# Two pieces of shared-expert work moved ahead of the routed experts, with the additions and weight loads that follow from it

## The reference

```python
x = x + xattn(layernorm(x), ctx, mask, Wq, Wk, Wv, Wo)
h = layernorm(x)                                     # 4096 rows of 512
topk_idx, topk_w = gate(h)                           # 4 of 32 experts a token, 2 of 4 groups
out = moe(h, topk_idx, topk_w, w1, w2, w3)           # 32 experts, inner width 256, 128 rows each
shared = silu(h @ shared_gate) * (h @ shared_up) @ shared_down   # inner width 512
x = x + out + shared
```

## Time and profile before

| | |
|---|---|
| median of 3 runs | 1642.79 us |
| the profiled execution, its own time | 1645.73 us |
| its span, first to last instruction | 1644.0 us |
| PE busy | 1602.1 us, 97% |
| DVE busy | 1216.7 us, 74% |
| ACT busy | 827.0 us, 50% |
| POOL busy | 818.7 us, 50% |
| mean share of the 16 DMA engines, 1397.75 to 1576.01 us | 0.93 |

### The profile page before, as it was taken

The page is one execution under the profiler, slowest core; times in us unless marked ns, Lnnn a source line. Parts: engine busy times, 40 slices in busy tenths (PEclk is TensorE's granted clock), DMA queues, the critical chain, the costliest instruction groups (busy, mean ns, idle before and its releaser), DMA issues. The chain is left out here.

```text
span 1644.0 us, 34926 instructions
## 1 busy us (share of the span) xinstructions
PE 1602.1 (97%) x12194; PEld 1149.3 (70%) x12194; DVE 1216.7 (74%) x3510; ACT 827.0 (50%) x2050; POOL 818.7 (50%) x1130
## 2 busy tenths in 40 slices
PE   7999999999999999999999999999999999999994
PEld 4767777777777686777777777777777777666641
DVE  7987676767767676767677778787787766687883
ACT  5764443534344443444354454544454443777782
POOL 3444554536354645445455564646464456354453
PEclk9999999999999999999999999999999999999997
DMA  8754433434334333434354545545444476899984
GB/s 242 186 142 84 82 81 78 96 67 98 69 88 72 88 76 78 85 78 85 69 120 79 105 96 114 113 87 108 91 108 87 104 260 181 266 280 292 301 209 59
DMA packets 395053, 205.69 MB, mean 125 GB/s; under 512 B 347888, under 2 KB 356080, under 8 KB 394880
## 3 DMA queue, kind: packets, MB, share of 16 engines
q1 hardware_dynamic: 380720, 181.32, 44.8%
q0 software_dynamic: 13600, 21.10, 6.9%
q10 hardware_dynamic: 560, 1.05, 0.2%
HBM read 87.67 MB, written 32.41 MB: 73 GB/s over the span
## 5 line engine op out<-in xcount | busy, mean ns | idle before, releaser
L980 ACT ACTIVATE arena<-arena,neg_max 128x256 f32<-128x256 f32 x512 | 253.7, 496 | 379.5 <-DVE neg_max L1297 319.0
L716 POOL TENSOR_SCALAR arena<-arena,prob_scale 128x256 f16<-128x256 f32 x384 | 183.4, 492 | 454.0 <-DVE prob_scale L1306 452.2
L1656 PE MATMUL ps_query<-xn_both,arena 128*128 128x256 f16 x1024 | 279.8, 273 | 1.5 <-DMA xn_both<-xn_half 1.5
L1657 PE MATMUL ps_query<-xn_both,arena 128*128 128x256 f16 x1024 | 279.8, 273 | 0.0
L1658 PE MATMUL ps_query<-xn_both,arena 128*128 128x256 f16 x1024 | 279.8, 273 | 0.0
L1297 DVE CUSTOM_DVE_ANT_0 arena<-ps_score,mask_add 128x256 f32<-128x256 f32 x512 | 186.7, 420 | 120.6 <-PE ps_score L1658 119.7
L1312 DVE SCALAR_TENSOR_TENSOR arena<-arena,prob_scale 128x256 f16<-128x256 f32 x384 | 231.7, 651 | 7.6 <-POOL arena L716 7.6
L1656 PE MATMUL ps_out<-arena,o_t 128*128 128x512 f16 x512 | 194.1, 379 | 4.2 <-DVE o_t L1317 4.2
L1657 PE MATMUL ps_out<-arena,o_t 128*128 128x512 f16 x512 | 194.0, 379 | 0.0
L1658 PE MATMUL ps_out<-arena,o_t 128*128 128x512 f16 x512 | 194.0, 379 | 0.0
L771 POOL DMA_INDIRECT slot_table<-entry,slot_at x128 | 132.9, 1039 | 48.1 <-issue 33.6
(11 more groups left out here) (341 smaller groups left out, 4067.8 us busy)
## 6 DMA issues: line engine op xcount, KB each, us to landing
arena<-w SPq DMA_DIRECT2D x96, 512.0 KB, 6.7
x_in<-x SPq DMA_DIRECT2D x15, 512.0 KB, 4.1
xn_rows<-xn_half SPq DMA_DIRECT2D x15, 512.0 KB
out_rows_dram<-x SPq DMA_DIRECT2D x30, 256.0 KB
ctx_in<-ctx_t SPq DMA_DIRECT2D x16, 256.0 KB, 3.0
weight_in<-wq SPq DMA_DIRECT2D x8, 512.0 KB, 5.1
weight_in<-wo SPq DMA_DIRECT2D x8, 512.0 KB, 4.4
arena<-arena SPq DMA_TRANSPOSE x256
```

The source lines that it names most:

```text
L716: pool.tensor_scalar(p_rows[:, c, 0, :], probs[:, c, :], prob_scale[:, c:c + 1], 1.0, ALU.mult, ALU.mult).then_inc(norm_hi, 1)
L980: act.activation(probs[:, c, :], probs[:, c, :], ACT.Exp, bias=neg_max[:, c:c + 1], scale=-1.0, accum_out=prob_sum[:, c:c + 1]).then_inc(e ...
L1656: pe.matmul(dst, a.hi, b.hi, start=start and n == 0, stop=False)
L1657: pe.matmul(dst, a.hi, b.lo, start=False, stop=False)
```

## The change

EARLY goes from 24 to 26: the pieces 24 and 25, both halves of the down product of late sequence 3, run ahead of expert 0, and every later piece runs beside an expert two earlier. Experts 22 to 31 are then without a piece. The rule for add_in is written anew, since sequence 3 has no piece beside an expert any more; its table becomes {4: (3,), 12: (4, 5), 22: (6, 7)}. Late sequences 1 and 2 become separate groups of additions, so that add_shared(2) now waits for the landing of add_shared(1), and piece 24 for that of add_shared(1) alone. POOL splits pieces up to EARLY - 1 in a loop; the two new ones are down pieces and need no split. SP loads the experts 6, 7 and 8 whole, one after the other, where it staggered the parts. DVE makes the low halves of expert 1 right after piece 11 and those of expert 2 behind pieces 14, 15 and 16.

```diff
--- before.py
+++ after.py
@@ -62,7 +62,7 @@
     PIECES += [("d", _n - 1, t) for t in range(TB)] if _n else []
     PIECES += [("u", _n, f) for f in range(2, FSB)]
 PIECES += [("d", len(LATE) - 1, t) for t in range(TB)]
-EARLY = 24
+EARLY = 26
 RAMP = 18
 NOT_BY_POOL = (10, 11, 14, 15, 16)
 BESIDE = {}
@@ -445,14 +445,14 @@
 
 
         additions = [("s", n) for n in range(1, 3)]
-        add_in = {max(e + e % 2, 4): ns for ns in ((3,), (4, 5), (6, 7)) for e, k in BESIDE.items()
-                  if PIECES[k] == ("d", ns[-1], TB - 1)}
+        staged_in = {PIECES[k][1]: e for e, k in BESIDE.items() if PIECES[k][0] == "d"} | {3: 0}
+        add_in = {max(staged_in[ns[-1]] // 2 * 2 + 2, 4): ns for ns in ((3,), (4, 5), (6, 7))}
         for e in range(2, E + 1, 2):
             additions += [("s", n) for n in add_in.get(e, ())]
             additions += [("x", e - 1), ("x", e - 2)]
         assert len(additions) == E + len(LATE) - 1
         adds_done, adds_before, total = {}, {}, 0
-        for kind, together in groupby(additions, key=lambda what: (what[0], what[1] // 2 if what[0] == "x" else 0)):
+        for kind, together in groupby(additions, key=lambda what: (what[0], what[1] // 2 if what[0] == "x" else min(what[1], 3))):
             together = list(together)
             size = 16 * len(together) * (TB if kind[0] == "s" else 1)
             for what in together:
@@ -622,9 +622,12 @@
             load_x2t(4)
 
 
-            for e in range(AHEAD - 2, E):
+            for e in range(AHEAD, AHEAD + HELD):
                 for part in range(3):
-                    if e + 2 - part >= AHEAD:
+                    load_expert(e, part)
+            for e in range(AHEAD, E):
+                for part in range(3):
+                    if e + 2 - part >= AHEAD + HELD:
                         load_expert(e + 2 - part, part)
                 if AHEAD <= e < AHEAD - 1 + KEPT:
                     load_x2t(e - AHEAD + 5)
@@ -751,7 +754,7 @@
                     pool.wait_ge(staged, TB * n + t + 1)
                     if t == 0:
                         pool.wait_ge(out_rows, 16 * TB * (LATE[n] + 1))
-                        if n > 2:
+                        if n > 1:
                             pool.wait_ge(added, adds_before["s", n])
                     pool.dma_start(out[r:r + P, :], shared_y[n % 2][t], accum_op=ALU.add).then_inc(
                         added if n else added_first, 16)
@@ -850,7 +853,7 @@
             add_shared(2)
             for e in range(4, 6):
                 gather(e)
-            for k in (22, 23):
+            for k in range(22, EARLY):
                 late_split(k)
             pool.wait_ge(out_rows, 16 * TB * B)
             pool.wait_ge(added_first, 16 * TB)
@@ -1607,16 +1610,12 @@
             pick(position)
             find_slots(z)
             piece_rest(10)
-            for k, e, part in ((11, 0, 2), (14, 1, 0), (15, 1, 1), (16, 1, 2)):
+            for k, lows in ((11, ((0, 2), (1, 0), (1, 1), (1, 2))), (14, ((2, 0),)), (15, ((2, 1),)), (16, ((2, 2),))):
                 piece(k)
-                if k > 11:
-                    expert_low(e, part)
                 piece_rest(k)
-                if k == 11:
+                for e, part in lows:
                     expert_low(e, part)
             piece(17)
-            for part in range(3):
-                expert_low(2, part)
             piece(20)
             dve.wait_ge(in_table, 16)
             dve.tensor_scalar(slot_weight[:, :], table[:, :, 1].bitcast(F32), 0.5 * GLU * GLU * HE_S / ROUTE_SCALE,
@@ -1625,7 +1624,7 @@
             dve.wait_ge(table_scaled, 2)
             dve.tensor_scalar(to_spare, row_f, spare_row[:, 0:1], -PAIR_S / EY_S, ALU.subtract, ALU.mult).then_inc(
                 table_scaled, 1)
-            for k in (21, 22, 23):
+            for k in range(21, EARLY):
                 piece(k)
             for e in range(E + 1):
                 if e < E:
```

## The result

The changed kernel took 1650.35 us (median of 20 runs, 1644.61 to 1656.67), the kernel before 1642.82 us beside it (20 runs, 1639.11 to 1648.58). The ratio is 1.0045, 95% interval 1.0035 to 1.0054: slower by 7.4 us. Forecast were +4.2 us and slower as the likeliest; the time lies inside the range of 1641.5 to 1651.0, at its upper end, and just outside the forecast's own range of 1644.5 to 1650.

What follows compares the result with a forecast made beforehand. From 1498.54 the serial chain of POOL's additions sets the end. Its links summed to a span of 1648.2 against 1644.0, + 4.2 us; added to the median 1642.79 this gave 1647.0 us, range 1641.5 to 1651.0.

Steps and rivals of the forecast that it cites:

- Two pieces ahead, + 5.18: PE in front of the experts: two down pieces of 2.59 us each start expert 0 5.18 us later, at 1402.93.
- Experts 22 and 23 without pieces, + 1.01: PE at experts 22 and 23: the pair takes 10.79 us against 9.78 of own work, losing 1.01 us.
- The chain never catches up: POOL's additions: each group starts later than its data from expert 10 on; backlog 7.0 us at experts 18 and 19.
- the first rival: Additions of experts 12 to 19: links fall to 12.33 us, the chain meets its data, end 1637.7; chance 0.20.
- a start by 1578: Sign in POOL's chain: sequences 6 and 7 starting by 1578, not near 1583, means it caught up and the forecast is wrong.
- The moved step takes nothing out of the chain: Shared step of sequences 6 and 7, expert 24 to 22: the chain must pass it all the same, no saving.
- The link behind the sequences 6 and 7, 9.73: Chain from the start of sequences 6 and 7 to pair 20 and 21: 9.73 us, 1583.1 to 1592.8.
- the link *to* the step: Chain from experts 18 and 19 to sequences 6 and 7: taken as 13.5 us, between 15.47 and 9.56.
- SP and DVE, cost 0: Earlier loads of experts 6 to 8 and moved low halves: no gain by themselves, no piece moved, cost 0.
- the third rival: PE at piece 24 stalls for piece 21's halves beyond 1.8 us of slack; 4 us late gives 1649.2; chance 0.15.
- The second rival (late links long by chance): Late chain links: ordinary ones 14.05, the one ahead of sequences 6 and 7 11.6; 1643.7, no change; chance 0.15.
- Links long by the load alone: Chain links between pairs: 14.52 us while weights stream in against 8.17 without, read as the effect of DRAM load.

Runs made afterwards that it cites:

- after: First profile of the changed kernel itself: the profiled execution took 1648.54 us; the kernel's median was 1650.35 us, ratio 1.0045 against before.
- e1: Changed kernel with SP's loads and DVE's low halves in the order of before: ratio 1.0023 against before, median 1650.35 us.
- e10: Changed kernel with POOL's split of piece 20 ahead of the four gathers and that of piece 21 between second and third: 1.0027, 1650.93 us.
- e3: Changed kernel once more, unedited, for its own time and a second profile: ratio 1.0043 against before, median 1653.43 us.
- e4: Changed kernel with both additions of every pair of experts issued back to back, no gather between: ratio 1.0016 against before, 1649.46 us.
- e5: Kernel before with both additions of every pair of experts issued back to back, no gather between: ratio 0.9976 against before, 1645.29 us.
- e7: Changed kernel without the additions of late sequences 6 and 7, their shared part missing from the output: ratio 0.9999 against before, 1650.87 us.
- e9: Kernel before once more, same code, for a second profile: one execution of 1641.85 us.
- e6: Changed kernel with the additions of sequences 6 and 7 back at expert 24, behind experts 20 and 21: ratio 1.0028 against before, 1654.17 us.
- e8: Kernel before with pair additions back to back and late sequences 4 to 7 added singly at experts 8, 14, 20, 24: 0.9963, 1644.54 us.

## Why the prediction was right, and too small

- **Two pieces ahead, + 5.18.** Held. Expert 0 starts 5.8 us later after the first late piece than before in after, stall of 1.51 us included, and 4.7 later in e1 and e10, which have no stall. From the first late piece to experts 8 and 9's addition it is 163.8 us against 159.1, + 4.7.
- **Experts 22 and 23 without pieces, + 1.01.** Held: from expert 22 to expert 24 it is 10.7 us on PE (1564.9 to 1575.6; forecast 10.79).
- **The chain never catches up.** Held in the profile of after, where every group from expert 10 on was later than its data, and not in e3, where the chain met its data at experts 16 to 19, as the first rival had it (in e4 and e5 as well, with pairs back to back). On the forecast's scale the sequences 6 and 7 started at 1583.1 in after and at 1577.0 in e3; the prediction itself called a start by 1578 a sign that it is wrong. Of the 6.2 us that e3 had won by then over after, 3.1 were left at the end: the longer links behind the step took the rest. The first rival's price, 9.3 us, was too high for that reason.
- **The moved step takes nothing out of the chain.** Held: it must still pass it, and without it (e7) the loss is gone.
- **The link behind the sequences 6 and 7, 9.73: the term that was mis-sized.** I took it from the earlier trace rows, where the step stood at expert 24, behind the last weights. At expert 22 it stands ahead of their end. Measured were 11.92 to 14.61, 13.3 on average over the five profiles, + 3.6 us. The prediction named this too as a sign of being wrong, links behind the step that are not 8 to 10 us. I had asked that question of the link *to* the step, and took 13.5 (measured 13.28 in after), but not of the link behind it, though the earlier trace rows have one for the same four transfers inside the weight stream: that of the sequences 4 and 5, 12.67.

That term does not account for the 7.4 us, since others fell by as much. The parts in us, for the five profiles with the sequences 6 and 7 together at expert 22 (after and e3 are the changed kernel itself, the others have one edit each):

| part | forecast | after | e3 | e1 | e4 | e10 | mean of five |
|---|---|---|---|---|---|---|---|
| first late piece to experts 8, 9 | 164.3 | 163.8 | 163.6 | 162.6 | 164.1 | 162.7 | 163.3 |
| to the sequences 6, 7 | 93.8 | 94.4 | 88.4 | 94.9 | 87.6 | 89.9 | 91.0 |
| link behind them | 9.7 | 11.9 | 12.9 | 14.4 | 14.6 | 12.7 | 13.3 |
| from there to the end | 55.4 | 53.6 | 55.8 | 55.0 | 54.8 | 54.6 | 54.8 |
| sum | 323.2 | 323.7 | 320.6 | 326.9 | 321.0 | 319.8 | 322.4 |

The sum was right to 1 us on average, and in after to 0.5, while its terms were off by up to 3.6 in either direction; that part is luck. The two profiles of the changed kernel average 322.2 us, the two of before (319.0 and, in e9, 317.1) 318.1: + 4.1, beside the forecast's + 4.2, though the profiles of one kernel differ by 2 to 3 us. The medians say 7.4. The profiled executions of the changed kernel were faster than its medians (1648.54 against 1650.35, 1649.75 against 1653.43), so where the other 3 us lie is open.

- **SP and DVE, cost 0.** Not held beside the two pieces: the slot table came later in every profile with the new orders, and PE stalled at piece 24 by 0.7 us (e3) and 1.51 us (after), as the third rival said from a slack of 1.8 us. In after PE reached piece 24 71.0 us after the first late piece (forecast 71.9) and the halves of piece 21 were ready after 72.3 (forecast 70.1). That rival and the forecast happened together; I had priced them as cases that exclude each other. Whether the new orders cost more than the stall is open.
- **The second rival (late links long by chance).** Half right as a caution: the profile of before was 2.9 us over the median, and e9 puts its time from the first piece 1.9 us lower.
- **Links long by the load alone.** The prediction set 14.52 us under load against 8.17 without and gave the difference to the load. But the pairs of 14.52 have a gather between their additions and those of 8.17 have none. Back to back and still under load a pair's link was 8.8 to 12.6 us, 11.0 on average, so a part of the difference goes with the gather.
- e6, which moves only the step back, gives back 0.15 to 0.17%, in the direction of the mis-sized term; its interval takes in no difference as well as the whole term, and its profile, of an execution 3.2 us over its median, is no shorter (326.4 us from the first late piece to the end). A finer split can't be had from these runs.

## What to carry to other kernels

Where a serial chain of transfers sets the end, measure for each link how long after its data it starts: where that never falls to nothing, work that arrives earlier wins little, and a step moved forward within the chain stays in it. Price a moved step, and what stands behind it, in the traffic of the new place, not of the old. Then shorten the links themselves (dependent pairs issued back to back, long steps split and spread to where the chain has slack), which here won 0.37% of the kernel before without touching the work of PE, DVE or ACT.

## What the runs showed of the hardware

- **A landing depends on when it happens.** From the end of the step's issue to the next addition it was 6.1 us before (1592.09 to 1598.18), 6.5 in e6, 8.3 in after and 10.8 in e1. An accumulating pair in the quiet last stretch lands in 4.4 us. The Trainium skill's page "DMA: Bandwidth & Descriptors" (Anatomy of one DMA) fits a transfer issued from POOL as 2.0 us and its bytes at 436 GB/s; for the 256 KB of one addition that is an estimate of 2.6 us from the last issue to the landing. The trace disagrees for these accumulating transfers, and the measured 4.4 decides.
- **A gather between two additions stretches a link by more than its issue.** While the weights stream in and the next pair is over 2.5 us late, links of a pair with a gather between its additions were 11.7 to 15.9 us (28 of them, 14.1 on average), back to back ones 8.8 to 12.6 (22, 11.0 on average), for gathers of 1.1 to 2.0 us.
- **One queue for gathers and for a waiting chain.** A late addition held a gather behind it in POOL's queue, and PE stood 4.0 us for it in e1.
- **The start differs between executions.** The first late piece started between 1323.0 and 1331.9 us in the fourteen profiles, with no change ahead of it. A part is the granted clock of the first 200 us, 1.00 in e9 and 0.97 in e6 (columns as above), whose first late pieces start at 1323.0 and 1329.3; but e8, with 0.98 there, starts at 1331.9, so it is not all:

```profile
0.00:200.00 200.00, 190.12 (x1419) 136.73 (x1420) 159.54 (x417) 112.11 (x270) 84.68 (x145) 1.00 0.61 151
```

```profile
0.00:200.00 200.00, 190.49 (x1391) 136.28 (x1392) 156.61 (x405) 109.57 (x261) 83.81 (x142) 0.97 0.59 148
```
